# One core, a decoder layer with a selective scan: scan weights and first residual moved in the load order, and a second scratch for batch 0's softplus

## The chip, the cores and the metric

The kernel runs on one core of a Trainium2 chip. The metric is the device time of one execution, in microseconds. Instruction names of engines: PE is the matrix engine (TensorE), with PEld for its weight loads; DVE is the vector engine, ACT the scalar (activation) engine, POOL is GpSimd, and SP is the engine whose queue issues all of this kernel's DMAs.

## What is computed

Four batches of 512 tokens with 512 channels go through one decoder layer, in float32. The reference, cut to its core:

```python
x = x + attention(layernorm(x))                 # 16 heads of 32, causal
x = x + ssm(ctx, layernorm(x))                  # selective scan over ctx, gated by x
x = x + ffn(layernorm(x))                       # ternarized weights, 512 -> 2048 -> 512

# ssm(hidden_states, z, ...):  512 channels, 16 states
x = einsum('ed,bld->bel', in_proj_w, hidden_states)
u = silu(causal_conv4(x) + conv_b)
x_dbl = einsum('ke,bel->bkl', x_proj_w, u)      # 16 rows for dt, 16 for B, 16 for C
delta = softplus(einsum('er,brl->bel', dt_proj_w, dt_lo) + dt_proj_b)
state = state * exp(delta * A) + (delta * u) * B_t      # along 512 tokens, for each state
y = (sum over states of state * C_t + D * u) * silu(z)
```

## The kernel before

Every kind of work has a name, and is cut into items: `("dt", b, et)` is the dt projection and softplus of batch b and channel block et (4 blocks of 128 channels), `("xproj", b)` the x projection, `("scan", j)` half a state of one batch, `("s", p, n)` a piece of the attention scores of slot p (two heads; 32 slots in all), `("rot", b, n, half)` a quarter of the q/k projection with its rotary turn. `follows(item)` (L428) says for each item which engine does which part of it, a cost in us for each part, and what it needs. `schedule()` gives each item a due time from tables (`SSM_FRONT`, `ATTN_END`, `PACE` and others), and `plan()` (L638) is a greedy list planner: it picks for each engine the item that can start first by those costs, and among items that can start within 0.3 us of each other the one with the smallest due time plus a weight of its kind. What it gives is a fixed order for each engine, `ORDER`, and the choice of the PSUM bank for each item; the engines then go through their lists in that order and wait on semaphores. So a changed need changes the order of everything after it, with the same tables. The planner also counts a few filler matmuls (L1582) ahead of a matmul group where it expects PE to wait.

The front of the network for batch 0 goes as follows. SP loads x in tiles of 128 tokens into two buffers (L1134), then identity and small constants ("basic", L1125), the first context and the input projection's weights (L1148, L1125), the first residual `xr` (L1189, 1 MB, needed by the first output projection's addition at L1915), further x tiles, the second context, two chunks of attention weights (L1121), and with them the rotary tables and the two weights of the scan, `xp_w` and `dt_w`. PE projects the context (L1604), ACT takes the last tap (L1425), DVE adds three taps (L1849), ACT does silu (L1430). PE projects u to x_dbl (L1613), ACT copies it (L1438), SP stores its B and C rows to HBM (L1160) and loads each state's row back over 128 partitions (`b_bc`, L1167). PE multiplies with dt_w (L1629).

The softplus of a block takes three slices of a scratch `tmp`: ACT writes relu and abs of the biased product (L1455, L1456), exp(-abs) over the abs (L1459), and ln(1 + that) (L1461). For batch 0 DVE makes delta from it with a correction for rounding (L1857 to L1863); for later batches POOL does (L1259 to L1265). There is one scratch, so ACT's next block waits until the delta before it is made (L1454), and the planner holds the dt matmul until then (L687). `du` = delta x u is on POOL (L1273).

The scan of half a state takes ACT's exp(delta x A) into two PSUM banks (L1377), POOL's product of du and B (L1248), one scan instruction on DVE (L1795); PE turns the state (L1708) and DVE adds it to y, weighed with C (L1817). ACT's next exp waits until the scan before has read the two banks.

Attention starts with the rotary work: PE (L1639), DVE (L1872 to L1880), POOL (L1279, L1280), ACT's rounding copy (L1467), POOL's residue (L1285), SP's store to HBM (L1156) and the loads of q and k (L1181). There is one buffer `hl` for it, so the next quarter waits for the store.

The feed-forward part (L1757 to L1777) follows when batch 3's attention is over, beside the last batch's scan, and ends the kernel.

Of the kernel before, what the change touches and what calls it, by code (L numbers as in the profile page):

```python
# [24 lines left out]
ALU = mybir.AluOpType  # L25
ACT = mybir.ActivationFunctionType
# [9 lines left out]
ET = DM // P  # L36
# [7 lines left out]
SLOTS = B * 8  # L44
# [372 lines left out]

def delta_by(b):

    return "pool" if b else "dve"  # L420
# [7 lines left out]
def follows(item):  # L428
# [4 lines left out]
    pe, act, dve, pool, sp = (lambda *x, e=e: (e, x) for e in ("pe", "act", "dve", "pool", "sp"))  # L433
    if kind == "xload":
        i = LT * a[0] + a[1]
# [4 lines left out]
    elif kind == "ln1b":  # L440
        b, t = a
# [5 lines left out]
    elif kind == "inproj":  # L447
        b, et = a
# [5 lines left out]
    elif kind == "xproj":  # L454
        b, = a
        yield "pe", 3.5, [act("silu", b, ET - 1), sp("wload", 1)]
        yield "act", 0.6, [pe(*item)] + ([sp("xproj", b - 1), pe("dt", b - 1, ET - 1), pe("ct", b - 1)] if b else [])
        yield "sp", 0.3, [act(*item)]
    elif kind == "ct":
        b, = a  # L460
        yield "pe", 0.3, [act("xproj", b)]
        yield "act", 0.3, [pe(*item)] + ([ht_last(b - 2)] if b >= 2 else [])
    elif kind == "bcload":
        i, = a
# [4 lines left out]
    elif kind == "delta":  # L469
        b, et = a  # L470
# [4 lines left out]
    elif kind == "du":  # L475
        b, et = a
        yield "pool", 1.3, [(delta_by(a[0]), ("delta", *a)), act("skip", b, et // 2), pe("xproj", b)]
    elif kind == "rot":
        b, n, half = a
# [9 lines left out]
    elif kind == "v":  # L489
        b, c, tt = a  # L490
        yield "pe", 3.5, [act("ln1b", b, LT - 1), sp("wload", CHUNK_OF[kind, b, c])]
        yield "act", 0.6, [pe(*item)] + ([pe(*reader_before(b, c))] if reader_before(b, c) else [])
    elif kind == "wload":
        c, = a
# [14 lines left out]
    elif kind == "pv":  # L509
        g, = a  # L510
        b = g // 4
# [7 lines left out]
    elif kind == "resid":  # L519
        b, = a  # L520
        yield "sp", 6, [sp("x2store", b - 1, t) for t in range(LT)] if 0 < b < B - 1 else \
            [pe("pv", SLOTS // 2 - 1)] if b else []
# [115 lines left out]
def plan():  # L638
# [29 lines left out]
    scratch, line, loaded = [], 0.0, "exp"  # L668
# [7 lines left out]
    def earliest(engine, item):  # L676

        at = 0.0
        for x in before[engine, item]:
            if x not in over:  # L680
                return None
            at = max(at, over[x])
        if (engine, item) in last_use:
            if not bank():
                return None
            at = max(at, bank()[0])
        if engine == "pe" and item[0] == "dt" and scratch:  # L687
            if scratch[-1] not in over:
                return None
            at = max(at, over[scratch[-1]])  # L690
        return at

    left = sum(len(items) for q in queues.values() for items in q.values())
    while left:
# [43 lines left out]
        if engine == "pe" and item[0] == "dt":  # L738
            scratch.append((delta_by(item[1]), ("delta", *item[1:])))
# [40 lines left out]
def layer_kernel(nc, t_in, out):  # L780
    sems = {}
    with ExitStack() as ctx:
# [236 lines left out]

        def delta_made(eng, b, et):  # L1020

            if b == 0:
                eng.wait_ge(delta_ready["dve"], et + 1)
            else:
                eng.wait_ge(delta_ready["pool"], ET * (b - 1) + et + 1)
# [16 lines left out]
        def bank(*item):  # L1042

            return ps[:, PLACE[item][0], :]
# [74 lines left out]
        def _(sp):  # L1119
# [3 lines left out]
            def load_consts(group):  # L1123
                for dst, src in CONSTS[group]:
                    sp.dma_start(dst[:], src).then_inc(const_in[group], 16)  # L1125

            for item in ORDER["sp"]:
# [9 lines left out]
                elif kind == "wload":  # L1137
# [4 lines left out]
                    if c < 2:  # L1142
                        load_consts(("rotary", "scan")[c])
                elif kind == "cload":
# [4 lines left out]
                    if b == 0:  # L1149
                        load_consts("inproj")  # L1150
                elif kind == "lo":
# [196 lines left out]
        def _(act):  # L1348
# [7 lines left out]
            for kind, *a in ORDER["act"]:  # L1356
# [91 lines left out]
                elif kind == "dt":  # L1448
# [4 lines left out]
                    if b or et:  # L1453
                        delta_made(act, *divmod(ET * b + et - 1, ET))  # L1454
                    nc.scalar.activation(tmp[:, 0, :], bank(kind, *a), ACT.Relu, bias=dt_b[:, et, :])  # L1455
                    nc.scalar.activation(tmp[:, 1, :], bank(kind, *a), ACT.Abs, bias=dt_b[:, et, :])\  # L1456
                        .then_inc(m_free["act"], 1)
                    act.wait_ge(m_free["act"], FREED[n][1])
                    own.done(nc.scalar.activation(tmp[:, 1, :], tmp[:, 1, :], ACT.Exp, scale=-1.0))  # L1459
                    own.settle()  # L1460
                    nc.scalar.activation(tmp[:, 2, :], tmp[:, 1, :], ACT.Ln, bias=1.0).then_inc(sp_ready, 1)  # L1461
# [319 lines left out]
        def _(dve):  # L1781
# [5 lines left out]
            for kind, *a in ORDER["dve"]:  # L1787
# [64 lines left out]
                elif kind == "delta":  # L1852
# [3 lines left out]
                    d = delta[b % 2][:, et, :]  # L1856
                    own.done(v.tensor_scalar(d, tmp[:, 1, :], 1.0, 1.0, ALU.add, ALU.subtract))  # L1857
                    own.settle()
                    own.done(v.tensor_tensor(d, tmp[:, 1, :], d, ALU.subtract))
                    own.settle()  # L1860
                    own.done(v.tensor_tensor(d, d, tmp[:, 2, :], ALU.add))
                    own.settle()
                    v.tensor_tensor(d, d, tmp[:, 0, :], ALU.add).then_inc(delta_ready["dve"], 1)  # L1863
# [244 lines left out]
```

## Time and profile before

| | us |
|---|---|
| median of 3 runs | 1136.7 (1135.46 to 1136.88) |
| the profiled execution's own time | 1134.5 |
| its span, first to last instruction | 1132.7 |
| PE busy | 1003.6 (89%) |
| DVE busy | 958.9 (85%) |
| ACT busy | 793.3 (70%) |
| POOL busy | 625.1 (55%) |

Busy time counts compute instructions; PE's includes the fillers, and its matmuls are pipelined, so a busy PE is not one at its peak. The shares are means over stages that have different limits: the head, a long middle with attention and scan side by side, and the feed-forward end. Idle time of an engine is put down to the instruction that ended it.

### The profile page before, as it was taken

Reading aid. Unit: us, or ns where it says so; the run is one execution under the profiler, and the core shown is the slowest. Engines: PE = TensorE matmul, PEld = TensorE weight load, DVE = VectorE, ACT = ScalarE, POOL = GpSimd, SP = SyncE. Lnnn points to the kernel's source line nnn. Section 1 sums busy time; section 2 is a strip of 40 time slices with the busy share of each in tenths; the row PEclk is TensorE's granted clock in tenths of the full one; section 3 lists DMA queues with packets and bytes.
Section 4 is the critical chain, followed back from the end, with each engine's and each line's share of the span. In section 5 each row is a group of like instructions: output and inputs, shape, how many; then the busy total and the mean of one; then the engine's idle time right before and its main releaser. Section 6 shows DMA issues by size and latency. Waiting matters only on the chain. (4 is left out here: it accounts for less than half of the span.)

```text
span 1132.7 us, 18945 instructions
## 1 busy us (share of the span) xinstructions
PE 1003.6 (89%) x6034; PEld 760.6 (67%) x6034; DVE 958.9 (85%) x1351; ACT 793.3 (70%) x1529; POOL 625.1 (55%) x509
## 2 busy tenths in 40 slices
PE   7998988999988999789899985887888998989997
PEld 5555666669664668556567664676767776878886
DVE  5758898996998869998986789899999999998654
ACT  4656756765786776888767696827988978984432
POOL 1369485554536796456738831569655655544401
PEclk9999999999988999899999986997899999989999
DMA  5325356364435545323555460420111110000000
GB/s 194 114 76 171 109 151 184 105 198 152 116 103 182 154 131 168 103 81 106 167 190 159 139 194 6 175 105 26 41 47 34 38 33 32 26 16 19 10 19 19
DMA packets 59360, 115.91 MB, mean 102 GB/s; under 512 B 8880, under 2 KB 13232, under 8 KB 58240
## 3 DMA queue, kind: packets, MB, share of 16 engines
q1 hardware_dynamic: 59264, 114.70, 32.4%
q8 instruction: 51, 0.84, 0.3%
q14 instruction: 45, 0.37, 0.1%
HBM read 90.42 MB, written 24.25 MB: 101 GB/s over the span
## 5 line engine op out<-in xcount | busy, mean ns | idle before, releaser
L1248 POOL TENSOR_TENSOR hb<-du,b_bc 128x1024 f32<-128x1024 f32 (+1 forms) x160 | 314.8, 1987 | 160.6 <-PE ps L1708 160.6
L1795 DVE TENSOR_TENSOR_SCAN hb<-ps,hb 128x1024 f32<-128x1024 f32 (+1 forms) x128 | 257.4, 2013 | 33.3 <-ACT ps L1377 20.0
L1377 ACT ACTIVATE ps<-delta,a_neg 128x511 f32<-128x511 f32 (+2 forms) x320 | 180.6, 600 | 79.5 <-DVE hb L1795 73.3
L1817 DVE SCALAR_TENSOR_TENSOR y_acc<-ps,ct,y_acc 128x512 f32<-128x512 f32 x256 | 181.2, 740 | 24.5 <-PE ps L1708 23.8
L1708 PE MATMUL ps<-ident,hb 128*128 128x128 f32 x1088 | 160.1, 288 | 43.8 <-DVE hb L1795 12.7
L1708 PEld LDWEIGHTS ps<-ident,hb 128*128 128x128 f32 x1088 | 127.8, 147 | 72.1 <-issue 14.2
L1487 ACT ACTIVATE p_q<-ps,m_col 128x512 f32<-128x512 f32 (+3 forms) x256 | 131.5, 530 | 20.9 <-DVE m_col L1892 12.2
L1639 PE MATMUL ps<-xn_t,w_ring 128*128 128x512 f32 x256 | 117.9, 604 | 0.8 <-DVE o_t L1908 0.6
L1766 PE MATMUL ps<-t_fc,xq_hi 128*128 128x512 f32 x256 | 106.2, 415 | 3.2 <-DVE hq_lo L2007 3.2
L1682 PE MATMUL ps<-ident,p_q 128*128 128x128 f32 x640 | 91.9, 287 | 14.4 <-ACT p_q L1487 7.2
L1503 ACT ACTIVATE p_t<-ps 128x512 f32<-128x512 f32 x160 | 88.2, 605 | 22.9 <-PE ps L1682 22.6
L1775 PE MATMUL ps<-t_pr,hq_hi 128*128 128x512 f32 x256 | 102.2, 399 | 1.9 <-DVE hq_lo L2007 1.9
L1766 PE MATMUL ps<-t_fc,xq_lo 128*128 128x512 f32 x256 | 101.9, 398 | 0.0
L1775 PE MATMUL ps<-t_pr,hq_lo 128*128 128x512 f32 x256 | 101.1, 395 | 0.0
L1892 DVE TENSOR_REDUCE m_col<-ps 128x1 f32<-128x512 f32 (+2 forms) x192 | 88.5, 501 | 8.1 <-PE ps L1667 7.0
L1682 PEld LDWEIGHTS ps<-ident,p_q 128*128 128x128 f32 x640 | 75.0, 147 | 28.5 <-ACT p_q L1487 9.2
L1663 PE MATMUL ps<-k_st,q_st 128*128 128x512 f32 (+3 forms) x256 | 76.5, 374 | 10.5 <-DVE y_acc L1817 7.8
L1639 PEld LDWEIGHTS ps<-xn_t,w_ring 128*128 128x128 f32 x256 | 46.9, 192 | 52.5 <-issue 50.0
L1582 PE MATMUL ps<-ident 128*128 128x128 f32 x478 | 67.4, 292 | 11.2 <-DMA small<-in_small 5.5
L1582 PEld LDWEIGHTS ps<-ident 128*128 128x128 f32 x478 | 59.1, 152 | 18.0 <-DMA small<-in_small 5.5
L1546 ACT ACTIVATE h_sb<-ps,fx 128x512 f32<-128x512 f32 x64 | 42.7, 686 | 30.1 <-PE ps L1766 28.5
L1565 ACT ACTIVATE h_sb<-h_sb,fh 128x1024 f32<-128x1024 f32 x32 | 38.4, 1236 | 30.9 <-POOL fh L1338 30.9
(151 smaller groups left out, 2016.5 us busy)
## 6 DMA issues: line engine op xcount, KB each, us to landing
w_ring<-in_w_attn SPq DMA_DIRECT2D x32, 512.0 KB, 3.7
qk_d<-hl SPq DMA_DIRECT2D x64, 256.0 KB
q_st<-qk_d SPq DMA_DIRECT2D x128, 128.0 KB, 2.8
b_bc<-bc_d SPq DMA_DIRECT2D x48, 256.0 KB, 3.9
k_st<-qk_d SPq DMA_DIRECT2D x64, 128.0 KB, 2.7
k_st<-qk_d SPq DMA_DIRECT2D x128, 64.0 KB, 2.3
x_in<-in_x SPq DMA_DIRECT2D x16, 256.0 KB, 2.9
raw_fc<-in_w_fc SPq DMA_DIRECT2D x4, 1024.0 KB, 9.2
```

The source lines that it names most:

```text
L1248: nc.gpsimd.tensor_tensor(piece_of(e, hi, lo).rearrange("p (a n) -> p a n", a=2), du[b % 2][:, 2 * h:2 * h + 2, lo:hi], b_bc[:, i % BC_RIN ...
L1377: ins = nc.scalar.activation(factors(j, hi, lo)[:, (hi - lo) * m + start:(hi - lo) * (m + 1)], delta[b % 2][:, et, lo + start:hi], ACT.Exp ...
L1487: ins = nc.scalar.activation(p_q[:, h, Q_AT[i]:Q_AT[i] + w], src[:, col:col + w], ACT.Exp, bias=m_col[:, i, h:h + 1], accum_out=z_sum[:, b ...
L1582: nc.tensor.transpose(bank(*item)[:, 0:P], ident[:], ident[:])
L1639: mm = nc.tensor.matmul(bank(kind, *a), w_ring[:, c % 2, d, P * half:P * half + P], xn_t[:, d, :], start=(d == 0), stop=(d == KD - 1))
L1682: mm = nc.tensor.transpose(dst[:, at:at + P], p_q[:, h, Q_AT[i] + P * jt:Q_AT[i] + P * jt + P], ident[:])
L1708: mm = nc.tensor.transpose(bank(kind, *a)[:, P * et:P * et + P], piece_of(2 * r + et // 2, hi, lo)[:, at:at + P], ident[:])
L1766: mm = nc.tensor.matmul(bank(kind, t, n), part[:, t % 2, d, :], t_fc[:, d, 512 * n:512 * n + 512], start=(d == 0 and m == 0), stop=(d == K ...
L1775: mm = nc.tensor.matmul(bank(kind, t), part[:, k, :], t_pr[:, k, :], start=(k == 0 and m == 0), stop=(k == FT - 1 and m == 1))
L1795: v.tensor_tensor_scan(h, d, h, 0.0, ALU.mult, ALU.add).then_inc(scan_done, 1)
L1817: v.scalar_tensor_tensor(out=y, in0=bank(kind, r, tb), scalar=ct[:, b % 2, tb, n:n + 1], in1=y, op0=ALU.mult, op1=ALU.add).then_inc(y_free ...
L1892: ins = v.tensor_reduce(m_col[:, i, h:h + 1], src[:, col:col + P * (i + 1)], AX.X, ALU.max, negate=True)
```

## The change

The planner and the kernel are changed together; the tables of due times and weights are the same. `xp_w` and `dt_w` are loaded right behind the input projection's weights instead of behind attention weight chunk 1, and the planner lets x_proj go when the first context's load is over. The first residual's load needs, for the planner, batch 0's store of B and C. Batch 0's softplus uses two scratches by turns: `tmp` for blocks 0 and 2, the buffer `gate` for 1 and 3. ACT then waits for the delta two blocks back, and the planner's rule for the dt matmul is the same. Batches 1 to 3 stay with `tmp`.

```diff
+def scratch_user(b, et):
+    i = ET * b + et
+    return None if i < 2 else divmod(i - 2 if b == 0 else i - 1, ET)
...
-        yield "pe", 3.5, [act("silu", b, ET - 1), sp("wload", 1)]
+        yield "pe", 3.5, [act("silu", b, ET - 1), sp("cload", 0)]
...
-            [pe("pv", SLOTS // 2 - 1)] if b else []
+            [pe("pv", SLOTS // 2 - 1)] if b else [sp("xproj", 0)]
...
-        if engine == "pe" and item[0] == "dt" and scratch:
-            if scratch[-1] not in over:
+        if engine == "pe" and item[0] == "dt" and scratch_user(*item[1:]):
+            user = scratch_user(*item[1:])
+            made = delta_by(user[0]), ("delta", *user)
+            if made not in over:
                 return None
-            at = max(at, over[scratch[-1]])
+            at = max(at, over[made])
...
+        def scratch(b, et):
+            return gate if b == 0 and et % 2 else tmp
...
-                    if c < 2:
-                        load_consts(("rotary", "scan")[c])
+                    if c == 0:
+                        load_consts("rotary")
...
                     if b == 0:
                         load_consts("inproj")
+                        load_consts("scan")
...
-                    if b or et:
-                        delta_made(act, *divmod(ET * b + et - 1, ET))
-                    nc.scalar.activation(tmp[:, 0, :], bank(kind, *a), ACT.Relu, bias=dt_b[:, et, :])
+                    if scratch_user(b, et):
+                        delta_made(act, *scratch_user(b, et))
+                    s = scratch(b, et)
+                    nc.scalar.activation(s[:, 0, :], bank(kind, *a), ACT.Relu, bias=dt_b[:, et, :])
```

The other three ACT instructions of `dt` and the four of DVE's `delta` read and write `s` in place of `tmp` in the same way.

## Rows read from the trace of the kernel before

**Rows 1.** Busy us (x instructions) in stretches: PE, PEld, DVE, ACT, POOL, clock, DMA, GB/s.
```profile
90.00:750.00 660.00, 582.14 (x3945) 427.73 (x3944) 569.60 (x744) 481.37 (x1070) 395.32 (x232) 0.95 0.46 142
750.00:1020.00 270.00, 235.23 (x1194) 196.18 (x1193) 261.01 (x404) 218.95 (x324) 163.28 (x196) 0.93 0.10 32
1020.00:1132.70 112.70, 106.10 (x541) 87.71 (x539) 72.60 (x123) 42.85 (x62) 30.75 (x50) 1.00 0.05 17
```

**Rows 2.** The chain that ended last, its first long piece: start us, us, what.
```profile
763.76 2.38 DVE stats L1921 x4
```

**Rows 3.** The stretches again, two of the head.
```profile
30.00:60.00 30.00, 29.37 (x120) 14.95 (x118) 23.10 (x33) 20.93 (x31) 11.29 (x8) 1.00 0.28 94
60.00:90.00 30.00, 28.38 (x134) 18.27 (x135) 17.79 (x21) 15.44 (x24) 20.87 (x11) 0.94 0.31 98
```

**Rows 4.** Timeline, x_proj: start us, us, engine, line, out<-in [idle before].
```profile
26.31 0.63 ACT L1430 ACTIVATE du<-du 128x512 f32<-128x512 f32 x1 [2.60 <-DVE du L1849]
...
29.62 3.60 PE L1639 MATMUL ps<-xn_t,w_ring 128*128 128x512 f32 x8
...
33.15 3.63 PE L1613 MATMUL ps<-du,xp_w 128*48 128x512 f32 x8
...
36.82 0.59 ACT L1438 ACTIVATE x_dbl<-ps 48x512 f32<-48x512 f32 x1 [3.87 <-PE ps L1613]
...
41.51 0.69 ACT L1455 ACTIVATE tmp<-ps,small 128x512 f32<-128x512 f32 x1 [1.69 <-PE ps L1629]
```

**Rows 5.** Timeline, softplus blocks and deltas of batch 0.
```profile
45.50 2.78 POOL L1285 TENSOR_TENSOR hl<-hl 128x1024 fp32r<-128x1024 f32 x1 [1.17 <-ACT hl L1467]
46.10 2.72 DVE L1863 TENSOR_TENSOR delta<-delta,tmp 128x512 f32<-128x512 f32 x1
...
48.92 0.69 ACT L1455 ACTIVATE tmp<-ps,small 128x512 f32<-128x512 f32 x1 [0.89 <-DVE delta L1863]
...
50.88 0.63 ACT L1461 ACTIVATE tmp<-tmp 128x512 f32<-128x512 f32 x1
...
62.92 0.69 ACT L1455 ACTIVATE tmp<-ps,small 128x512 f32<-128x512 f32 x1 [0.44 <-DVE delta L1863]
...
65.54 0.43 DVE L1857 TENSOR_SCALAR delta<-tmp 128x512 f32<-128x512 f32 x1 [1.52 <-ACT tmp L1461]
...
67.45 0.69 DVE L1863 TENSOR_TENSOR delta<-delta,tmp 128x512 f32<-128x512 f32 x1
```

**Rows 6.** Timeline, the first scans and POOL's second product.
```profile
58.04 2.29 DVE L1795 TENSOR_TENSOR_SCAN hb<-ps,hb 128x1024 f32<-128x1024 f32 x1 [1.67 <-POOL hb L1248]
...
74.05 2.36 POOL L1248 TENSOR_TENSOR hb<-du,b_bc 128x1024 f32<-128x1024 f32 x1
...
76.51 2.29 DVE L1795 TENSOR_TENSOR_SCAN hb<-ps,hb 128x1024 f32<-128x1024 f32 x1 [4.98 <-POOL hb L1248]
...
85.76 2.29 DVE L1795 TENSOR_TENSOR_SCAN hb<-ps,hb 128x1024 f32<-128x1024 f32 x1 [0.80 <-ACT ps L1377]
89.50 2.29 DVE L1795 TENSOR_TENSOR_SCAN hb<-ps,hb 128x1024 f32<-128x1024 f32 x1 [1.45 <-ACT ps L1377]
```

**Rows 7.** Timeline, two entries of SP's queue.
```profile
11.97 0.98 SPq L1134 DMA_DIRECT2D x_in<-in_x  x2
...
48.30 3.63 SPq L1156 DMA_DIRECT2D qk_d<-hl  x4
```

**Rows 8.** DMA issues up to 80 us: size, median us from issue to landing.
```profile
xr<-in_x SPq DMA_DIRECT2D x1, 1024.0 KB, 7.9
...
xp_w<-in_xp_w SPq DMA_DIRECT2D x1, 96.0 KB, 5.5
```

**Rows 9.** The instructions on tmp: ns min/median/max, first and last start.
```profile
L1863 DVE TENSOR_TENSOR delta<-delta,tmp x4: 692/692/2722, 46.1 to 67.5; 128x512 f32<-128x512 f32 x4
```

**Rows 10.** Two lines' instructions: first residual addition, and the scores (same columns).
```profile
L1915 DVE TENSOR_TENSOR xr<-ps,xr x12: 665/691/692, 273.2 to 630.1; 128x512 f32<-128x512 f32 x12
...
L1663 PE MATMUL ps<-k_st,q_st x256: 218/388/797, 95.7 to 707.2; 128*128 128x512 f32 x32, 128*128 128x128 f32 x32, 128*128 128x256 f32 x32, 128*128 128x384 f32 x32
```

More of the change, by code:

```diff
@@ L667, in plan @@
     held = [[("dve", ("scan", PIECES - 1))] if n in DA_BANKS else [] for n in range(8)]
-    scratch, line, loaded = [], 0.0, "exp"
+    line, loaded = 0.0, "exp"
     out = {engine: [] for engine in queues}
@@ L737, in plan @@
             over[engine, item] = at + us + 0.2
-        if engine == "pe" and item[0] == "dt":
-            scratch.append((delta_by(item[1]), ("delta", *item[1:])))
     return out, place, fill
@@ L1452, in _ @@
                     act.wait_ge(m_full, n + 1)
-                    if b or et:
-                        delta_made(act, *divmod(ET * b + et - 1, ET))
-                    nc.scalar.activation(tmp[:, 0, :], bank(kind, *a), ACT.Relu, bias=dt_b[:, et, :])
-                    nc.scalar.activation(tmp[:, 1, :], bank(kind, *a), ACT.Abs, bias=dt_b[:, et, :])\
+                    if scratch_user(b, et):
+                        delta_made(act, *scratch_user(b, et))
+                    s = scratch(b, et)
+                    nc.scalar.activation(s[:, 0, :], bank(kind, *a), ACT.Relu, bias=dt_b[:, et, :])
+                    nc.scalar.activation(s[:, 1, :], bank(kind, *a), ACT.Abs, bias=dt_b[:, et, :])\
                         .then_inc(m_free["act"], 1)
                     act.wait_ge(m_free["act"], FREED[n][1])
-                    own.done(nc.scalar.activation(tmp[:, 1, :], tmp[:, 1, :], ACT.Exp, scale=-1.0))
+                    own.done(nc.scalar.activation(s[:, 1, :], s[:, 1, :], ACT.Exp, scale=-1.0))
                     own.settle()
-                    nc.scalar.activation(tmp[:, 2, :], tmp[:, 1, :], ACT.Ln, bias=1.0).then_inc(sp_ready, 1)
+                    nc.scalar.activation(s[:, 2, :], s[:, 1, :], ACT.Ln, bias=1.0).then_inc(sp_ready, 1)
                 elif kind == "hi":
@@ L1855, in _ @@
                     dve.wait_ge(sp_ready, ET * b + et + 1)
-                    d = delta[b % 2][:, et, :]
-                    own.done(v.tensor_scalar(d, tmp[:, 1, :], 1.0, 1.0, ALU.add, ALU.subtract))
+                    d, s = delta[b % 2][:, et, :], scratch(b, et)
+                    own.done(v.tensor_scalar(d, s[:, 1, :], 1.0, 1.0, ALU.add, ALU.subtract))
                     own.settle()
-                    own.done(v.tensor_tensor(d, tmp[:, 1, :], d, ALU.subtract))
+                    own.done(v.tensor_tensor(d, s[:, 1, :], d, ALU.subtract))
                     own.settle()
-                    own.done(v.tensor_tensor(d, d, tmp[:, 2, :], ALU.add))
+                    own.done(v.tensor_tensor(d, d, s[:, 2, :], ALU.add))
                     own.settle()
-                    v.tensor_tensor(d, d, tmp[:, 0, :], ALU.add).then_inc(delta_ready["dve"], 1)
+                    v.tensor_tensor(d, d, s[:, 0, :], ALU.add).then_inc(delta_ready["dve"], 1)
                 elif kind == "rot" and a[2] == 0:
```

## The prediction

> **What bounds the kernel now.** I read busy time by stretch first, to see where an engine still has idle time that earlier work could fill. The vector engine (DVE) is busy 569.6 of 660 us (86%) from 90 to 750, and 261.0 of 270 us (97%) from 750 to 1020; only in the last 113 us is it TensorE (PE), at 94% [rows 1]. So from about 90 us on the kernel runs near the capacity of DVE, with PE close behind (88% from 90 to 750, part of it filler matmuls). The chain of waits starts only at 763 us, on DVE, and says nothing of the head [rows 2]. What the head can give is DVE's idle time there: it is busy 23.10 us from 30 to 60 and 17.79 from 60 to 90, so 60 - 40.9 = 19.1 us are idle [rows 3].
>
> Next the timeline of the head, to see why. Batch 0's u is ready when the fourth silu ends, 26.31 + 0.63 = 26.94 us, but x_proj's matmuls (L1613) start at 33.15, behind the first rotary chunk's (L1639, from 29.62), since the planner holds x_proj until weight chunk 1 has landed. x_dbl is copied at 36.82, and the first dt waits again behind the second rotary half, so softplus begins at 41.51 [rows 4]. Then the four softplus blocks go one at a time through one scratch: ACT starts the first at 41.51, the second at 48.92, the fourth at 62.92, and the last delta ends at 67.45 + 0.69 = 68.14 [rows 4, 5]. The first scan starts at 58.04, the second only at 76.51, after POOL's rotary pair and its product (dbu, 74.05) [rows 6]. Between them DVE has one scan in 18 us.
>
> **Part 1, x_proj released by the first context's load.** The planner's need becomes the silu and cload(0). x_proj then moves from 33.15 to about 27.0, 6.1 us earlier; the bound on the other side is 0, if another matmul group is put ahead of it. x_dbl's copy goes from 36.82 to about 30.7. From that copy to the first softplus are 4.7 us now, 3.7 of them under the second rotary half's matmuls [rows 4]; a shorter group would stand there instead (four matmuls of the context projection, by the rotary's eight in 3.6 us some 1.8), so I take 2.8 for 4.7, and the first softplus starts at 33.5 instead of 41.51: 8 us. xp_w takes 5.5 us to land and is issued, with dt_w, near 4 us, right behind the first context and in_w: it is there long before 27, and SP's next entry is an x load that waits for PE until 11.97, so the two issues delay nobody [rows 7, 8]. Weight chunks 0 and 1 may now be issued before the second context; the rotary matmuls at 29.62 show no wait for a DMA as it is [rows 4], so that is worth 0.
>
> **Part 2, two scratches.** A block is four ACT instructions (48.92 to 50.88 + 0.63 = 51.51: 2.59 us) and four DVE ones (65.54 to 68.14: 2.60) [rows 5]. With one scratch they alternate: four blocks are at least 4 x 5.19 = 20.8 us, and were 26.6 (41.51 to 68.14), so 5.8 us of other work and waits lay between. With two, ACT does a block while DVE does the one before: 5 x 2.6 = 13 us, plus what lies between (convolutions, silu and the table loads about it, copies). I take 5 us of it, as now: last delta at 33.5 + 13 + 5 = 51.5, against 68.14, so 16 to 17 us earlier; the bounds are 8 (only part 1) and 21 (nothing in between). The second scan then starts near 58 instead of 76.5, if POOL, which is free between its few rotary instructions, gives dbu its turn. The gate buffer that serves as scratch is first needed when batch 0's gates are made, some 200 us later: 0.
>
> **Part 3, the first residual after x_proj.** Its 1 MB took 7.9 us from issue to landing [rows 8], behind the small constants that PE and ACT wait for, so moving it is worth 0 there, at most some tenths. It is read first by the first output projection's addition, at 273.2 us [rows 10], so a load issued near 35 to 40 us is covered by over 200 us; SP's queue has no new wait, it only stands behind bc_d's store, which waits anyway. What it may hit are b_bc's first loads and the first q/k store (48.30): bound 0 to 7.9 us on that store, and I take 0 since the DMA engines are 28% busy from 30 to 60 us [rows 3, 7].
>
> **What reaches the end.** Once they run, the early scans follow each other at 3.74 us (85.76, 89.50) [rows 6], 7.5 us a state; in the 18.5 us won, 2.5 states could run, at most 18.5 us of DVE work. But it has to fit into idle time: all of it is 19.1 us, and if the stretch 30 to 90 became as dense as 90 to 750 (86%), 10.9 us would be recovered. Up to the first delta near 36 us nothing new comes to DVE, so I take 8. Of this I let 0.8 through, since DVE is 86% busy in the middle and the rest of its time goes by PE and by transfers that this does not bring forward: 6.5 us. Below: 0, if the middle is bound by the attention's chain; above: 19.1. From 750 on DVE is full and PE after it, so what is won at 750 is kept.
>
> The sum against the profiled execution (span 1132.7, time 1134.5): 1134.5 - 6.5 = 1128.0. The median of the runs, 1136.7, is 2.2 above it; on that scale the forecast is 1130.
>
> **A rule against the change.** DVE's last addition of delta(0,0) took 2.72 us at 46.10 instead of 0.69, while POOL's L1285 ran from 45.50 to 48.28; it ended 0.5 us behind it [rows 5, 9]. The Trainium skill, "SBUF — State Buffer", section "Who interferes with whom", says that a DVE instruction with two SBUF inputs contends with a GpSimd instruction that reads SBUF, and that the second one to issue blocks until the first is over. By that rule, the trace agrees: L1863's other three took 0.69.
>
> **The rivals.**
> *Collisions of DVE and POOL (no change).* With deltas back to back, POOL's products du run beside the next block's additions, and its rotary work falls among them too. Three more collisions like the one seen (2.72 - 0.69 = 2.03 each) make 6.1 us: 1130 + 6 = 1136. For it: the one long row. Against: only one of L1863's four was hit [rows 9], and a stretched DVE instruction costs nothing where DVE would be idle. With it I count that the planner puts other matmuls ahead of x_proj, so that the change does not do what it says.
>
> *The attention starts later (slower).* The first rotary matmuls at 29.62 go behind x_proj (3.6 us), and the chain from them to the first scores at 95.7 runs through POOL, ACT, the store at 48.30, the second pair's store and the q/k loads [rows 4, 7, 10]. If the residual's load also holds up the store, the delay is 3.6 to 11.5 us. It decides if the 32 slots (95.7 to 707.2, 19.1 us each) are paced by that chain and not by DVE, because the end of attention gates the feed-forward's start. Price: 1136.7 + 3.6 = 1140 to 1148, likely 1142. Against: the second rotary pair stands on DVE among deltas that will be gone. For: the planner is greedy, so with its start times shifted it makes another order with the same due times throughout, and 14% of DVE's time in the middle is idle already [rows 1].
>
> *All of it (much faster).* The idle time is refilled to the middle's density or beyond and nothing is lost: 10.9 to 19.1 us, so 1118 to 1126, likely 1123.
>
> **How the numbers follow.** Forecast (1125 to 1134.4, at 1130): 0.47. No change (1134.4 to 1139, at 1136): 0.17. Attention later (1139 to 1148, at 1142): 0.25. All of it: 0.11. Measurement tells 0.2% (2.3 us) from no change, so below 1134.4 is faster: 0.47 + 0.11 = 0.58; same 0.17; slower 0.25. For 8 in 10, half of the last case and a third of the slow one stay outside: 1121 to 1144. The likeliest case's own range is 1125 to 1134.
>
> **What would show it.** Right: L1613 first at about 27 us; ACT's L1455 four times within 13 to 18 us, from about 33; the second scan before 62; DVE busy over 45 of 60 us from 30 to 90; the first scores no later than 95.7; the last addition of wo (L1915) about 6 us before now. Wrong in part 1 if L1613 still stands behind L1639; in part 2 if L1863 is long more than once or ACT's blocks are still over 6 us apart; in part 3 if b_bc or the q/k store lands late. The prediction fails as a whole if the head is shorter by this and DVE's idle time from 90 to 750 grows over 90 us by as much.

## The result, and the profile of the changed kernel

The changed kernel takes 1158.2 us (median of four runs, 1156.7 to 1160.3) against 1136.6: 1.0195 times as long, with a 95% interval of [1.0179, 1.0211]. It is 2% slower, where 0.6% faster was forecast; the time lies outside the range of 1121 to 1144. The profiled execution has a span of 1158.5 us, 25.8 more than the 1132.7 of before, at a mean granted clock of 0.948 against 0.953. It was the longest of the four (1160.3 us); by the medians the difference is 21.7 us. All start times and delays below are of single profiled executions, so they carry some us of such spread. Line numbers below are those of the new code, 12 or 13 further down: L1626 is x_proj (L1613 before), L1468 softplus (L1455), L1870 to L1876 delta, L1808 the scan (L1795), L1260 POOL's product for it (L1248), L1721 the turn of the state (L1708), L1830 the addition to y (L1817), L1652 the q/k projection (L1639), L1885 and L1892 the rotary turn on DVE, first and second half (L1872, L1879), L1291 and L1292 its part on POOL, L1480 and L1297 the split into two parts on ACT and POOL (L1467, L1285), L1168 the q/k store (L1156), L1676 the scores (L1663), L1928 the output projection's addition (L1915).

The page of the profile, busy us of each engine, and the filler matmuls, and below it the filler matmuls of before:

```profile
PE 1016.6 (88%) x6091; PEld 771.7 (67%) x6091; DVE 964.5 (83%) x1351; ACT 793.5 (68%) x1529; POOL 624.5 (54%) x509
...
L1595 PE MATMUL ps<-ident 128*128 128x128 f32 x535 | 75.0, 293 | 10.0 <-DMA small<-in_small 5.3
```

```profile
L1582 PE MATMUL ps<-ident 128*128 128x128 f32 x478 | 67.4, 292 | 11.2 <-DMA small<-in_small 5.5
```

The 57 more fillers are the only instructions that PE has more (6091 against 6034). They aren't the cause by their number: the kernels e3 and e7 below have 467 and 452, fewer than before, and are slower than it.

The stretches of the changed kernel (columns as in [rows 1]), and below them three of the kernel before:

```profile
30.00:90.00 60.00, 54.05 (x226) 33.42 (x225) 48.21 (x57) 37.28 (x55) 27.62 (x17) 0.94 0.29 89
90.00:200.00 110.00, 97.92 (x626) 72.23 (x625) 79.56 (x111) 66.69 (x160) 72.70 (x42) 0.92 0.49 144
200.00:300.00 100.00, 90.62 (x618) 67.95 (x617) 77.62 (x92) 63.04 (x153) 49.68 (x28) 0.98 0.46 140
...
90.00:750.00 660.00, 578.42 (x3824) 422.24 (x3823) 545.80 (x707) 466.00 (x1036) 384.52 (x214) 0.94 0.45 137
```

```profile
30.00:90.00 60.00, 57.75 (x254) 33.22 (x253) 40.89 (x53) 36.36 (x54) 32.16 (x19) 0.97 0.29 96
90.00:200.00 110.00, 96.43 (x684) 69.11 (x683) 96.33 (x130) 76.71 (x185) 75.37 (x44) 0.98 0.51 152
200.00:300.00 100.00, 95.57 (x639) 73.74 (x638) 82.92 (x111) 65.27 (x160) 54.92 (x29) 1.00 0.48 143
```

DVE does 7.3 us more in the head (48.21 against 40.89), as meant, and then 16.8 us less from 90 to 200 and 5.3 less from 200 to 300. From 90 to 750 its idle time grows from 90.4 to 114.2 us, by 23.8, nearly all of the 25.8 us. Of that, 22.1 us (16.8 + 5.3) fall ahead of 300.

The timeline of the head shows what comes earlier and what comes later (start us, us, engine, line, out<-in):

```profile
26.61 5.09 PE L1626 MATMUL ps<-du,xp_w 128*48 128x512 f32 x8
31.74 0.59 ACT L1450 ACTIVATE x_dbl<-ps 48x512 f32<-48x512 f32 x1 [3.90 <-PE ps L1626]
34.73 0.69 ACT L1468 ACTIVATE tmp<-ps,small 128x512 f32<-128x512 f32 x1
...
46.96 3.70 PE L1652 MATMUL ps<-xn_t,w_ring 128*128 128x512 f32 x8
47.07 0.69 ACT L1468 ACTIVATE gate<-ps,small 128x512 f32<-128x512 f32 x1 [0.91 <-PE ps L1642]
49.65 2.28 DVE L1808 TENSOR_TENSOR_SCAN hb<-ps,hb 128x1024 f32<-128x1024 f32 x1
...
53.74 0.69 DVE L1876 TENSOR_TENSOR delta<-delta,gate 128x512 f32<-128x512 f32 x1
54.35 0.69 DVE L1892 TENSOR_TENSOR hl<-ps,sin 128x512 f32<-128x512 f32 x1
55.75 1.28 POOL L1291 TENSOR_TENSOR hl<-hl 128x512 f32<-128x512 f32 x1
58.21 4.68 POOL L1260 TENSOR_TENSOR hb<-du,b_bc 128x1024 f32<-128x1024 f32 x2
58.42 1.04 ACT L1480 ACTIVATE hl<-hl 128x1024 fp32r<-128x1024 f32 x1
62.22 2.28 DVE L1808 TENSOR_TENSOR_SCAN hb<-ps,hb 128x1024 f32<-128x1024 f32 x1
62.83 2.37 POOL L1297 TENSOR_TENSOR hl<-hl 128x1024 fp32r<-128x1024 f32 x1
```

In the kernel before, the second rotary half took this way, and its last two steps are L1285 at 45.50 [rows 5] and the store at 48.30 [rows 7]:

```profile
36.72 3.70 PE L1639 MATMUL ps<-xn_t,w_ring 128*128 128x512 f32 x8
...
40.45 0.69 DVE L1879 TENSOR_TENSOR hl<-ps,sin 128x512 f32<-128x512 f32 x1 [1.70 <-PE ps L1639]
...
44.36 1.06 ACT L1467 ACTIVATE hl<-hl 128x1024 fp32r<-128x1024 f32 x1 [0.15 <-POOL hl L1280]
```

The scan's side came as forecast: x_proj at 26.6, the fourth softplus block at 47.1, the last delta done at 54.4, the second scan at 62.2 instead of 76.5. The attention's side pays for it. Its matmuls stand at 46.96 instead of 36.72, its turn on DVE behind the last delta (54.35 instead of 40.45), and on POOL two of the scan's products (from 58.21, 4.68 us together) stand ahead of L1297, which starts at 62.83 instead of 45.50. The stores of q and k, in the changed kernel and then in the kernel before, the rest of them:

```profile
65.23 3.48 SPq L1168 DMA_DIRECT2D qk_d<-hl  x4
95.51 3.40 SPq L1168 DMA_DIRECT2D qk_d<-hl  x4
...
198.69 3.42 SPq L1168 DMA_DIRECT2D qk_d<-hl  x4
...
288.59 3.41 SPq L1168 DMA_DIRECT2D qk_d<-hl  x4
```

```profile
78.74 3.47 SPq L1156 DMA_DIRECT2D qk_d<-hl  x4
...
178.21 3.42 SPq L1156 DMA_DIRECT2D qk_d<-hl  x4
...
261.68 3.45 SPq L1156 DMA_DIRECT2D qk_d<-hl  x4
```

And the two lines of [rows 10], with that of the last additions of the output projection (ns min/median/max, first and last start):

```profile
L1676 PE MATMUL ps<-k_st,q_st x256: 218/389/795, 112.8 to 733.3; 128*128 128x512 f32 x32, 128*128 128x128 f32 x32, 128*128 128x256 f32 x32, 128*128 128x384 f32 x32
...
L1928 DVE TENSOR_TENSOR xr<-ps,xr x12: 666/692/692, 296.8 to 656.2; 128x512 f32<-128x512 f32 x12
L1928 DVE TENSOR_TENSOR xr_last<-ps,xr_last x4: 659/676/678, 778.7 to 787.6; 128x512 f32<-128x512 f32 x4
```

The delay is there with the first store (+16.9 us): +16.8 at the second, +17.1 at the first scores, then +12.9 and +11.9 at the third and fourth store (131.31 and 160.32 against 118.37 and 148.43), +20.5 at the fifth, +26.9 at the eighth (the last of batches 0 and 1), +23.6 at the first residual addition, +26.1 at the last one (787.6 against 761.5), +25.8 at the end. Behind the eighth store the two kernels take the same time to the end, 871.0 and 869.9 us. That fits their lists: the planner gave every engine another order from the head on, and the same order again, item for item, from the first output projection on. So the question is about 300 us of re-ordered work, and whether the first store's delay makes all of it. That the delay shrinks to 11.9 and jumps to 20.5 at the fifth store, the first of batch 1, says that it isn't simply passed on.

### The profile page after: what moved, and what is told of

Its sections match the earlier page's. It is cut to its first block and busy times, and to the rows that moved or that the text cites. A ratio compares the mean times of both kernels' runs of the same rounds, so it can differ in the third digit from the quotient of the medians.

```text
span 1158.5 us, 19050 instructions
## 1 busy us (share of the span) xinstructions
PE 1016.6 (88%) x6091; PEld 771.7 (67%) x6091; DVE 964.5 (83%) x1351; ACT 793.5 (68%) x1529; POOL 624.5 (54%) x509
## 5 line engine op out<-in xcount | busy, mean ns | idle before, releaser
L1260 POOL TENSOR_TENSOR hb<-du,b_bc 128x1024 f32<-128x1024 f32 (+1 forms) x160 | 315.2, 1990 | 165.2 <-PE ps L1721 160.4
L1808 DVE TENSOR_TENSOR_SCAN hb<-ps,hb 128x1024 f32<-128x1024 f32 (+1 forms) x128 | 257.4, 2013 | 27.4 <-ACT ps L1389 20.1
L1830 DVE SCALAR_TENSOR_TENSOR y_acc<-ps,ct,y_acc 128x512 f32<-128x512 f32 x256 | 181.3, 741 | 35.9 <-PE ps L1721 35.1
L1721 PE MATMUL ps<-ident,hb 128*128 128x128 f32 x1088 | 161.2, 290 | 53.8 <-DVE hb L1808 23.6
L1721 PEld LDWEIGHTS ps<-ident,hb 128*128 128x128 f32 x1088 | 129.3, 148 | 81.7 <-DVE hb L1808 18.2
L1500 ACT ACTIVATE p_q<-ps,m_col 128x512 f32<-128x512 f32 (+3 forms) x256 | 131.5, 530 | 24.8 <-DVE m_col L1905 18.4
L1652 PE MATMUL ps<-xn_t,w_ring 128*128 128x512 f32 x256 | 118.8, 607 | 1.4 <-DVE hl L1886 0.8
L1595 PE MATMUL ps<-ident 128*128 128x128 f32 x535 | 75.0, 293 | 10.0 <-DMA small<-in_small 5.3
L1676 PE MATMUL ps<-k_st,q_st 128*128 128x512 f32 (+3 forms) x256 | 75.7, 371 | 9.1 <-DVE y_acc L1830 5.4
L1652 PEld LDWEIGHTS ps<-xn_t,w_ring 128*128 128x128 f32 x256 | 47.6, 195 | 54.0 <-issue 51.0
L1595 PEld LDWEIGHTS ps<-ident 128*128 128x128 f32 x535 | 66.9, 153 | 16.2 <-DMA small<-in_small 5.3
L1291 POOL TENSOR_TENSOR hl<-hl 128x512 f32<-128x512 f32 x16 | 20.4, 1276 | 88.6 <-DVE hl L1893 88.5
```

The costliest lines, as they stand in the source:

```text
L1260: nc.gpsimd.tensor_tensor(piece_of(e, hi, lo).rearrange("p (a n) -> p a n", a=2), du[b % 2][:, 2 * h:2 * h + 2, lo:hi], b_bc[:, i % BC_RIN ...
L1500: ins = nc.scalar.activation(p_q[:, h, Q_AT[i]:Q_AT[i] + w], src[:, col:col + w], ACT.Exp, bias=m_col[:, i, h:h + 1], accum_out=z_sum[:, b ...
L1595: nc.tensor.transpose(bank(*item)[:, 0:P], ident[:], ident[:])
L1652: mm = nc.tensor.matmul(bank(kind, *a), w_ring[:, c % 2, d, P * half:P * half + P], xn_t[:, d, :], start=(d == 0), stop=(d == KD - 1))
L1721: mm = nc.tensor.transpose(bank(kind, *a)[:, P * et:P * et + P], piece_of(2 * r + et // 2, hi, lo)[:, at:at + P], ident[:])
L1808: v.tensor_tensor_scan(h, d, h, 0.0, ALU.mult, ALU.add).then_inc(scan_done, 1)
```

## The experiments

Start times in us, each from one profiled execution; "to the end" is the span less the eighth store's start. Ratios are to the kernel before, timed beside each kernel.

| kernel | store 1 | store 2 | store 5 | store 8 | first scores | first addition | span | to the end | time, ratio |
|---|---|---|---|---|---|---|---|---|---|
| before | 48.3 | 78.7 | 178.2 | 261.7 | 95.7 | 273.2 | 1132.7 | 871.0 | 1 |
| after | 65.2 | 95.5 | 198.7 | 288.6 | 112.8 | 296.8 | 1158.5 | 869.9 | 1.0195 [1.0179, 1.0211] |
| e1 first store held | 63.6 | 84.7 | 183.6 | 268.1 | 102.1 | 279.5 | 1138.8 | 870.7 | 1.0058 [1.0035, 1.0081] |
| e9 second store held | 46.8 | 94.9 | 191.8 | 275.1 | 111.1 | 286.6 | 1146.5 | 871.4 | 1.0139 [1.0117, 1.0161] |
| e2 two scratches, order of before | 49.1 | 76.9 | 178.8 | 262.7 | 93.9 | 274.2 | 1133.7 | 871.0 | 0.9991 [0.9973, 1.0009] |
| e6 late residual, order of before | 47.2 | 76.0 | 175.5 | 259.2 | 94.6 | 270.7 | 1133.0 | 873.8 | 0.9995 [0.9974, 1.0015] |
| e3 two scratches alone | 50.4 | 86.3 | 189.2 | 269.9 | 103.2 | 281.3 | 1142.3 | 872.4 | 1.0065 [1.0040, 1.0090] |
| e5 x_proj alone | 51.0 | 74.6 | 176.6 | 260.5 | 91.6 | 271.9 | 1131.5 | 871.0 | 0.9971 [0.9953, 0.9989] |
| e4 x_proj and residual | 51.3 | 76.6 | 187.7 | 273.7 | 93.4 | 281.9 | 1143.7 | 870.0 | 1.0094 [1.0063, 1.0125] |
| e8 after, residual early | 65.0 | 95.6 | 195.2 | 288.6 | 114.0 | 297.5 | 1162.6 | 874.0 | 1.0203 [1.0151, 1.0255] |
| e10 after, old order from 220 | 66.2 | 95.2 | 196.9 | 280.1 | 112.2 | 291.5 | 1150.7 | 870.7 | 1.0170 [1.0137, 1.0203] |
| e7 after, rotary first | 54.7 | 83.9 | 176.9 | 272.8 | 100.2 | 282.6 | 1144.4 | 871.6 | 1.0082 [1.0055, 1.0110] |
| e11 e7, old order from 100 | 55.5 | 84.7 | 181.7 | 266.7 | 100.5 | 278.2 | 1139.4 | 872.7 | 1.0068 [1.0046, 1.0089] |
| e12 x_proj, two scratches | 52.6 | 76.2 | 175.4 | 259.4 | 94.8 | 270.9 | 1130.7 | 871.3 | 0.9985 [0.9970, 1.0000] |

One thing holds in all rows: from the eighth store to the end it is 870 to 874 us, whatever was done ahead of it. My theory was that the first store's delay passes through the attention's start to the end; the rivals were the new order itself (worse in other places), the residual's DMA, and collisions of DVE and POOL.

**e1: the first store held, nothing else.** The kernel before; SP waits ahead of the store for seven small copies, one after another.

```diff
 elif kind == "lo":
+    for k in range(7 if (b, n) == (0, 0) else 0):
+        sp.dma_start(idle_d, t_in["ident"]).then_inc(idled, 16)
+        sp.wait_ge(idled, 16 * (k + 1))
```

> The kernel before, every engine's order unchanged, but SP holds the first q/k store (issued at 48.30 us before, at 65.23 us in the changed kernel) behind seven small copies from HBM to HBM, each waited for, some 17 us in all. Theory A, that the start of attention sets the end: the first scores go from 95.7 to about 112 and the end follows one for one or more, 1150 to 1160 us. Theory B, that DVE's capacity sets the pace and the changed kernel lost its time elsewhere (its new order after the head): the hold is taken up by other work, under 5 us, so 1137 to 1141 us.

The first store came 15.3 us later, the second only 6.0:

```profile
63.62 3.45 SPq L1161 DMA_DIRECT2D qk_d<-hl  x4
84.74 3.37 SPq L1161 DMA_DIRECT2D qk_d<-hl  x4
...
268.08 3.45 SPq L1161 DMA_DIRECT2D qk_d<-hl  x4
```

The scores were 6.4 us later, the span 6.1, the time 0.6% longer. So the first store had 9 us of slack (15.3 - 6.0), and what the second one lost reached the end whole. The first store alone doesn't make the 25.8 us; the second is 16.8 us late in the changed kernel.

**e9: the second store held.** As e1, with `(b, n) == (0, 1)`; SP again does nothing else in that time.

> The kernel before with the seven copies ahead of the second q/k store (78.74 us before, 95.51 in the changed kernel) instead of the first. Holding the first cost 15.3 us at that store, 6.0 at the second store and 5.9 us at the end. Theory D, that the end follows the second store and the first scores one for one whatever the scan has done: both move by 14 to 16 us and the time is 1149 to 1154 us. If the scan, which is not held and can run ahead, takes up part of it, the time is below 1146 us.

```profile
46.84 3.58 SPq L1161 DMA_DIRECT2D qk_d<-hl  x4
94.88 3.44 SPq L1161 DMA_DIRECT2D qk_d<-hl  x4
...
275.14 3.44 SPq L1161 DMA_DIRECT2D qk_d<-hl  x4
```

```profile
90.00:200.00 110.00, 85.30 (x569) 61.92 (x570) 84.63 (x117) 70.42 (x173) 70.68 (x42) 0.91 0.54 155
```

The second store was 16.1 us later, the first scores 15.4, the eighth store 13.5, the span 13.8, and the time 1.4% longer. With the order and the scan of before, and only the attention's start held up, DVE's busy time from 90 to 200 falls from 96.33 to 84.63: 11.7 of the 16.8 us that it falls by in the changed kernel. This is the chain that the end hangs on, nearly one for one. SP's queue is held up too in these two kernels, with whatever stands behind the store; that share isn't told apart.

**e2: two scratches, the order of before.** The changed kernel, but the planner's three rules are the old ones, so that every list is that of before; the loads and the scratches are new. One rule of the three:

```diff
-        if engine == "pe" and item[0] == "dt" and scratch_user(*item[1:]):
-            user = scratch_user(*item[1:])
+        if engine == "pe" and item[0] == "dt" and ET * item[1] + item[2]:
+            user = divmod(ET * item[1] + item[2] - 1, ET)
```

> The changed kernel's instructions and waits (two scratches, scan weights behind the first context), but the planner's rules of before, so every engine's order, bank and filler count is that of before, the residual's place too. Theory A, that only the place of the first rotary work in the order costs time: first q/k store at 48 to 49 us, time within 3 us of before, 1134 to 1138 us. Theory B, that the second scratch or the early load of the scan's weights costs in itself (collisions of DVE and POOL, DMA traffic): slower by 3 us or more.

No change: 0.9991 [0.9973, 1.0009]. The scratch costs nothing and, while the lists stay, gives nothing.

**e3: two scratches alone, with the order that they bring.** The changed kernel, with the needs and the loads of x_proj and the residual as before:

```diff
-        yield "pe", 3.5, [act("silu", b, ET - 1), sp("cload", 0)]
+        yield "pe", 3.5, [act("silu", b, ET - 1), sp("wload", 1)]
...
-            [pe("pv", SLOTS // 2 - 1)] if b else [sp("xproj", 0)]
+            [pe("pv", SLOTS // 2 - 1)] if b else []
```

> Only the two scratches, with their planner rule; the loads and the needs of x_proj and of the first residual are those of before. Theory A reads the end from the first q/k store and from batch 0's first output projection addition (273.2 us before, 296.8 in the changed kernel). If the second scratch alone makes the softplus blocks push the rotary work back, the store is past 55 us and the time 1145 to 1158 us; if it is the earlier x_proj that does, the store stays near 49 us and the time is 1130 to 1140 us. Theory C, that any new order with the same tables costs some 10 us or more wherever the store falls: 1147 us or more with the store near 49 us.

0.65% slower. The first store is hardly later (50.4), the second 7.6 us, the eighth 8.2, the span 9.6. It is the planner that turns the scratch into a loss: it sees that the softplus blocks can run one behind the other, and puts the last one ahead of the second rotary chunk. The delay isn't one piece here either: 2.6 us at the fourth store (151.06 against 148.43), 11.0 at the fifth.

**e4 and e5: the loads, with and without the residual's need.** Both are the changed kernel with one scratch (`return None if i < 1 else divmod(i - 1, ET)` in `scratch_user`, `tmp` for all). e5 has besides:

```diff
-            [pe("pv", SLOTS // 2 - 1)] if b else [sp("xproj", 0)]
+            [pe("pv", SLOTS // 2 - 1)] if b else []
```

> Only the loads and the needs of x_proj and of the first residual are changed; one scratch as before. Theory A: with one scratch the gaps between softplus blocks leave room for the rotary work; if the earlier x_proj alone pushes the rotary work back the store is past 55 us and the time 1145 us or more; if both parts are needed for the loss, the store is within 3 us of 48.3 and the time 1133 to 1142 us. Theory C, that any new order costs: 1147 us or more with the store near 48 us.

> Only the scan weights' load behind the first context and x_proj's need of cload(0); the residual stays first, one scratch. The planner then gives another order only up to some 62 us, the same from the second rotary chunk on. Theory D, that the order between about 40 and 280 us decides, and that what is before it only shifts it: the time moves as the second q/k store does (78.74 us before), by 0 to -3 us, 1133 to 1138 us. Theory C, that any new order of the head costs: slower by 5 us or more.

e5 is 0.3% faster, 0.9971 [0.9953, 0.9989]. Its order is that of before again from about 62 us on, its second store 4.1 us earlier, its eighth 1.2, its span 1.2. How much of what the second store wins gets through isn't shown: by the spans it is 1.2 us of 4.1, by the times 3.3 us (0.3% of 1138), and the time of the kernel before, which that ratio goes by, had a median of 1138.5 in this round and of 1135.1 to 1137.3 in the others. e4 differs from e5 by one need and is 0.9% slower than the kernel before. Its second store is still earlier than in the kernel before (76.6), its fourth too (141.8 against 148.4), then the fifth is 9.5 us late and the eighth 12.0:

```profile
187.67 3.40 SPq L1168 DMA_DIRECT2D qk_d<-hl  x4
...
273.69 3.42 SPq L1168 DMA_DIRECT2D qk_d<-hl  x4
```

The lists show what changed between the fourth store and the fifth: all five pieces of slot 4's scores now stand ahead of the matmuls of batch 1's first rotary chunk, second half. In e3 three of them do, in the changed kernel three more turns of the scan's state, and the delay jumps between these two stores there too, by 8.4 and 8.6 us. In e9 and e1, with the order of before, it doesn't (14.0 and 13.6 us; 6.2 and 5.4). That these places cost the time is an inference; no run changes them alone.

**e6: is it the residual's transfer or its place in the plan?** The kernel before, its list of SP changed by hand, all other lists kept:

```diff
+ORDER["sp"].remove(("resid", 0))
+ORDER["sp"].insert(ORDER["sp"].index(("bcload", 1)) + 1, ("resid", 0))
```

> The kernel before with one entry of SP's list moved: the first residual's load stands behind the second row's load, near 41 us, instead of at 3.5 us. All other orders are kept. In the run with the load changes alone the time rose by 9 us. Theory D, that this came from the new order which the planner makes when the residual no longer fills its model of the DMA line: within 2 us of before, 1135 to 1139 us. Theory E, that the 1 MB itself collides with b_bc, the weight chunk and the first q/k store: the first q/k store's landing and the second store move by up to 8 us, and the time is 1139 to 1145 us.

```profile
40.21 0.43 SPq L1191 DMA_DIRECT2D xr<-in_x  x1
...
47.21 3.81 SPq L1158 DMA_DIRECT2D qk_d<-hl  x4
```

0.9995 [0.9974, 1.0015]: the 1 MB issued at 40.2, 7 us ahead of the first store, costs nothing. The loss of e4 is that of the order. The planner counts 6 us of its model's DMA line for the residual; with that moved, the x tiles and weight chunks behind it come early in its model, and it lays out the work of the first 300 us in another way.

**e7: the rotary work ahead of softplus.** The changed kernel; the first dt of batch 0 needs the second rotary half's matmuls:

```diff
-        yield "pe", 0.9, [act("xproj", a[0])]
+        yield "pe", 0.9, [act("xproj", a[0])] + ([pe("rot", 0, 0, 1)] if a[0] == 0 else [])
```

> The changed kernel, but the planner lets batch 0's dt matmuls go only when PE has done both halves of the first rotary chunk. Theory D: the first store returns from 65 to about 49 us and the second from 95.5 to about 80, and the time to 1130 to 1145 us, by how the eighth q/k store falls (261.7 us before, 288.6 in the changed kernel; the end has come 870 to 872 us behind it in each kernel so far). If the two scratches cost time by themselves it stays above 1150 us.

1.0082 [1.0055, 1.0110]: 14.1 us of the span come back out of 25.8. The first store is at 54.7 instead of 65.2, and the sixth at 210.33, 1.3 us ahead of before (211.65). But the seventh and eighth are late again, by 6.5 and 11.2 us:

```profile
272.84 3.44 SPq L1168 DMA_DIRECT2D qk_d<-hl  x4
```

In this list the matmuls of the fourth rotary chunk of batch 1, those ahead of the eighth store, stand behind three turns of the scan's state and two pieces of the scores of slot 10 that they stood ahead of before (they start at 251.95, against 241.10). That is a second loss, made behind a sixth store that was not late.

**e8: the changed kernel with the residual early.** Edit as the last one of e5, with both scratches.

> The changed kernel with the residual's load back ahead of the second pair of x tiles, in the planner too. Theory D: with x_proj early and two scratches the softplus blocks still stand ahead of the first rotary chunk's second half, so the first store stays past 60 us and the time at 1150 to 1160 us. If the residual's place is what starts the loss, the store is below 52 us and the time below 1145 us.

1.0203 [1.0151, 1.0255], the first store at 65.0, the eighth at 288.6: nothing came back that can be told from the spread (the interval is 1% wide). Each re-ordering cause is enough for a loss: the second scratch alone 0.65% (e3), the residual's need beside x_proj's 1.2% (e4 against e5), the second scratch beside x_proj's need 2.3% (e8 against e5).

**e10 and e11: how much is made where.** The planner runs with the old rules and with the new ones; every list is then the new order of those items that the old one began before 220 us of the planner's own time (e10) or, with e7's need, before 100 us (e11), and the old order from there on.

```diff
+HEAD = {e: [x for x in items if BEGAN[e, x] < 220] for e, items in OLD_ORDER.items()}
...
+MIXED = {e: [x for x in NEW_ORDER[e] if x in HEAD[e]] + OLD_ORDER[e][len(HEAD[e]):] for e in HEAD}
+ORDER, PLACE, FILLS = plan(MIXED)
```

> The changed kernel, but from the point that the planner calls 220 us on (the first transposes of slot 6, batch 0) every engine's order is that of before; up to there it is the changed kernel's. It asks how much of the loss is made behind that point. In the changed kernel the fifth q/k store is 20.5 us behind before's, the eighth 26.9. Theory D: the later order's part, 6 us, goes, and the loss of the first part stays: eighth store near 281 us, time 1150 to 1155 us. If most of the loss is made in the second part of batch 0, the time is below 1146 us.

> The changed kernel with the dt matmuls held until PE has done the first rotary chunk, as in the run with the rotary first, and from the planner's 100 us on (the first scores) the order of before. There the first scores came at 100.2 us and the time was 1146.4. Theory D: with before's order behind, the eighth store follows the second (83.9 us, 5.2 later than before) and does not fall back to 272.8: near 266 us, time 1139 to 1143 us. If the order behind the first scores does not matter, the time stays at 1144 to 1149 us.

```profile
196.91 3.43 SPq L1185 DMA_DIRECT2D qk_d<-hl  x4
...
280.05 3.44 SPq L1185 DMA_DIRECT2D qk_d<-hl  x4
```

With the old order from 220 on, the delay at the fifth store is 18.7 us, at the eighth 18.4, at the end 18.0. So some 18 us are made by the fifth store, and nothing is added behind it; in the changed kernel's profile 6.4 us are, from the fifth store to the eighth (20.5 to 26.9). By the times that part is smaller and not certain: 1.0170 [1.0137, 1.0203] against 1.0195 [1.0179, 1.0211], medians of 1153.4 and 1158.2 us. e11 has the delay of its second store, 6.0 us, still at the eighth (5.0) and at the end (6.7), as e1 had: with the old order behind it, a late second store is passed on and nothing is added.

**e12: both scratches on e5.** Two scratches, the residual early, and the planner's old rule for the scratch, which gives exactly e5's lists.

> The run with x_proj's load and need alone (second store 74.6 us, 1133.3 us), all orders kept, plus the second scratch in the kernel only. Theory D: with the order kept, ACT's waits for deltas fall but the matmuls stay where they are, so the second store is within 2 us of 74.6 and the time 1130 to 1135 us. If the second scratch has a cost of its own, from collisions of DVE and POOL, it is 1136 us or more.

0.9985 [0.9970, 1.0000], not told apart from e5. The best of the kernels tried is e5, x_proj's need and its weights with the first context, and nothing more: 0.3% in its own round.

## Why the prediction was wrong

**The steps of the head held, nearly in size.** x_proj started at 26.6 (forecast 27.0), the first softplus at 34.7 (33.5), the last delta was done at 54.4 (51.5), the second scan came at 62.2 (58, and the mark was 62); DVE was busy 48.2 of 60 us, where over 45 was the mark. x_proj's matmuls took 5.09 us, not 3.63 [rows 4]: the mean granted clock was 0.71 from 26.6 to 31.7 us, against 1.00 from 33.1 to 36.7 before; from the copy to the first softplus were 3.0 us (31.74 to 34.73) where I had 2.8. The marks behind the head failed: the first scores came at 112.8 and not by 95.7, the last residual addition 26.1 us later and not 6 earlier. The sign that I had given for a failure as a whole is what came: a shorter head, and more idle time of DVE from 90 to 750 us, by 23.8.

**"What reaches the end" failed in its premise.** I took DVE's idle time as what the kernel lacks, and idle time refilled as time gained: 8 us recovered (7.3 seen), 0.8 of it let through. Behind 200 us nothing is left of it. Eight scans had begun by 100 us instead of six (L1808 and L1795 in windows from 30), by 200 us 18 instead of 20, by 300 us 32 instead of 35. What is late at the end of the head is not the scan, it is the attention, and 86% busy was the mean of an engine that waits for two streams. Where one of them starts late, the middle loses DVE time that the other doesn't refill: e9 shows it with nothing else changed. The waits of DVE from 90 to 200 us say which work was missing (engine, line, what it waited for: us, times, longest), first of the changed kernel, then of before:

```profile
DVE y_acc L1830 <- PE ps L1721: 11.2, 3, 7.0
DVE hl L1885 <- PE ps L1652: 7.2, 3, 4.1
```

```profile
DVE hl L1872 <- PE ps L1639: 0.8, 2, 0.6
...
DVE y_acc L1817 <- PE ps L1708: 0.3, 1, 0.3
```

In its fixed list DVE stands at an addition to y for up to 7.0 us, and at rotary work behind late matmuls, while other work waits in line.

**The slow rival had the mechanism, and its price was mis-sized.** I gave it 0.25 and 3.6 to 11.5 us: x_proj's matmuls ahead of the rotary's, and at most the residual's load. The matmuls were the small part. By its own words the chain "runs through POOL, ACT, the store": I didn't count what the early softplus and scan put ahead of it on those queues. Counted with the rows above, the second half's matmuls move by 10.2 us (36.72 to 46.96), DVE's step by 13.9 (behind four deltas and a scan), ACT's by 14.1, and POOL's L1297 by 17.3, since two products, 4.68 us together, stand between. The delay at the first scores, 17.1 us, is 5.6 more than the most I had allowed. Its sentence against, that deltas "will be gone", was the wrong way round: the blocks had been spread out by the one scratch and let rotary work in between; drawn together they shut it out. Its decision point was right: what that chain loses ahead of the first scores reaches the end (e9).

**"From 750 on what's won is kept" held, for a loss.** Here the end follows the eighth store by 870 to 874 us in every kernel, so what moved the end was settled ahead of 300 us; DVE's capacity behind 90 us, which I had taken as the bound, didn't take up the delay. What paces the part behind the eighth store none of these runs tests. That the greedy planner makes another order I had named as a reason for the rival, and gave it no price: one need changed in it costs 12.2 us of span (e4 against e5).

**Part 3, the residual.** As a transfer it costs 0 (e6), as forecast. As a need it costs 1.2% where nothing but x_proj's need is changed beside it (1.0094 against 0.9971), and nothing that can be told apart in the whole change (e8), where the softplus blocks have re-ordered the work already. I had priced only its DMA.

**Collisions.** The rival fell. They did occur:

```profile
40.03 1.46 POOL L1285 TENSOR_TENSOR du<-delta,du 128x512 f32<-128x512 f32 x1 [3.13 <-DVE delta L1876]
40.40 1.64 DVE L1872 TENSOR_TENSOR delta<-gate,delta 128x512 f32<-128x512 f32 x1
...
44.93 2.35 POOL L1260 TENSOR_TENSOR hb<-du,b_bc 128x1024 f32<-128x1024 f32 x1
45.01 2.55 DVE L1870 TENSOR_SCALAR delta<-tmp 128x512 f32<-128x512 f32 x1 [0.32 <-ACT tmp L1474]
```

That is 0.9 us (1.64 for 0.69) and 2.1 (2.55 for 0.43) of DVE time beside POOL's products, 3.1 in all, against the 2.0 of the one of before [rows 5]. e2 and e12, with the two scratches too, show no loss.

**What stays open.** Where the loss behind the fifth store is made, item by item, was only located (the last rotary chunk of batch 1, in the lists of e7 and of the changed kernel), not tested alone. In e7 and e11 the first store is still at 54.7 and 55.5; ACT's rounding copy is at 50.14 in e7 and 50.97 in e11 instead of 44.36, behind two softplus blocks instead of one, and I take these for the cause, without a run. Of the 18 us by the fifth store, the delay of the second store accounts for some 14 (16.8 by e9's 13.8 out of 16.1, an estimate); the rest isn't separated from the order between. With each order the planner also chooses PSUM banks and filler counts anew, and the granted clock fell with it (0.98 to 0.92 from 90 to 200 us); neither is told apart from the order. In the whole execution PE was busy 13.0 us more (1016.6 against 1003.6), 7.6 of them fillers, so some 5 us of slower matmuls are in it.

## What to carry to other kernels

Before a step is brought forward, follow the chain that sets the pace of the next stage through every in-order queue that the step uses, and count on each one what will now stand ahead of it: here no instruction but fillers was added, and the chain lost 17 us. Idle time of a busy engine is a gain only if that engine's work is what ends last; hold up one transfer of a suspected chain in the old kernel and see how much of it arrives at the end, which one run answers. Where a planner writes the order, a changed need is a new order: run the code's change with the old order kept, and the order alone, since here the parts that cost nothing in themselves (e2, e6) cost 0.7% (e3) and 1.2% (e4 against e5) through the plan.

## What the runs showed of the hardware

A DVE instruction with a single SBUF input was held up as well: the 128x512 TENSOR_SCALAR L1870 took 2.55 us instead of 0.43, started 0.08 us behind POOL's 2.35 us product and ended 0.28 after it. I had expected this of the additions with two inputs only. The Trainium skill, "SBUF — State Buffer", section "Who interferes with whom", counts tensor_scalar among the operations that can enter a mode with two ports and then contend with GpSimd; the trace agrees with that. The granted clock from 90 to 200 us was 0.98 before, 0.92 in the changed kernel and 0.91 in e9, where PE was busy 97.9 and 85.3 us: these are means over stretches at either level. In e9, PE waited 13.3 us for the load of k ahead of the first scores; the clock was 0.61 from 97 to 111, with PE busy 0.81 us, and 0.50, the lower of its two levels (1.2 GHz), from 111 to 115, with the scores running. In the changed kernel the mean was lower though PE was no less busy over the stretch than before (96.4 us). And a 1 MB load issued 7 us ahead of the first q/k store cost no time that can be measured (e6).
